# Fused image and text embedding, window attention and routed experts: two image differences of GpSimd move from slot 12 to the front of a step

## The reference, cut to what matters

```python
# x: (16, 1, 256, 256) images, x_txt: (16, 77) token ids
out = conv_general_dilated(x, KERNEL, ...)       # two 2x2 kernels: differences along the two diagonals
h = clip(sum(abs(out), axis=1), 0, 1)            # (16, 256, 256): 256 rows of a picture become 256 tokens
h = concatenate([h, take(weight, x_txt)], 1)     # 16 batches of 333 tokens, width 256
h = h + attention(layernorm(h))                  # 16 heads of 16, windows of 128 tokens, stride 64, averaged
h = h + experts(layernorm(h))                    # top 2 of 8 SwiGLU experts, 256 -> 512 -> 256
```

## Time and profile before

| what | value |
|---|---|
| median of 3 runs | 1242.64 us (1241.91 to 1243.94) |
| profiled execution, its own time | 1235.95 us |
| its span | 1233.8 us |
| mean granted clock of TensorE | 0.987 of full speed |
| busy: PE, PEld, DVE, ACT, POOL | 93%, 77%, 68%, 57%, 48% of the span |
| PE, slices of 31 us | 9 tenths or more from the third to the last but one, save 8, 7 and 8 about where the steps end |
| POOL and ACT in the last 15 slices | 2 to 3 tenths, and 1 tenth |

### The profile page before, as it was taken

The page is one execution under the profiler, slowest core; times in us unless marked ns, Lnnn a source line. Parts: engine busy times, 40 slices in busy tenths (PEclk is TensorE's granted clock), DMA queues, the critical chain, the costliest instruction groups (busy, mean ns, idle before and its releaser), DMA issues.

```text
span 1233.8 us, 34479 instructions
## 1 busy us (share of the span) xinstructions
PE 1146.1 (93%) x10510; PEld 944.6 (77%) x10511; DVE 837.9 (68%) x4279; ACT 707.0 (57%) x1979; POOL 595.6 (48%) x751
## 2 busy tenths in 40 slices
PE   2499999999999999999998798999999999999995
PEld 1366766676667667666766698999999999999995
DVE  3488899899989899989888774444444444444442
ACT  1399999999999999999999721111111111111110
POOL 7655656765676567656653362223232332323232
PEclk9799999999999999999999998999999999999998
DMA  4654446554554355434535332232333323233332
GB/s 134 180 162 122 139 136 188 142 147 131 153 144 114 96 151 147 111 99 129 148 99 173 112 101 45 47 47 47 48 47 50 47 47 47 47 47 49 49 47 30
DMA packets 98394, 123.31 MB, mean 100 GB/s; under 512 B 15544, under 2 KB 87416, under 8 KB 95192
## 3 DMA queue, kind: packets, MB, share of 16 engines
q1 hardware_dynamic: 75880, 89.96, 26.7%
q0 software_dynamic: 18576, 24.47, 12.0%
q10 hardware_dynamic: 3808, 7.34, 1.9%
HBM read 69.35 MB, written 46.07 MB: 94 GB/s over the span
## 4 chain that ended last, share of the span: by engine, by line
PE 70%; DVE 7%; ACT 7%; POOL 7%; issue 4%; SPq 2%; DMA 1%; ACTq 0%; POOLq 0%; DVEq 0%
PE t_bank L1197 13%; PE s_bank L1197 13%; PE o_bank L1212 13%; PE m_bank L1245 7%; PE t_bank L1284 6%; PE o_bank L1300 5%; ACT probs L741 4%; PE s_bank L1273 4%; DVE probs L980 3%; PE m_bank L1239 3%; PE m_bank L1397 2%; PE m_bank L1186 2%; PE o_bank L1259 1%; PE o_bank L1409 1%; ACT probsT L734 1%
## 5 line engine op out<-in xcount | busy, mean ns | idle before, releaser
L741 ACT ACTIVATE probs<-probs,neg_max 128x128 f32<-128x128 f32 x1280 | 402.4, 398 | 2.1 <-DVE neg_max L980 2.1
L980 DVE CUSTOM_DVE_ANT_0 probs<-s_bank,nbias 128x128 f32<-128x128 f32 x1280 | 293.4, 284 | 56.6 <-PE s_bank L1273 51.2
L699 ACT ACTIVATE v_all<-s_bank 128x512 f32<-128x512 f32 x91 | 54.4, 598 | 284.5 <-PE s_bank L1197 284.4
L1284 PE MATMUL t_bank<-ident,probs 128*128 128x128 f32 x1280 | 194.1, 274 | 0.2 <-ACT probs L741 0.2
L1212 PE MATMUL o_bank<-stacks,v_all 128*128 x728 | 172.7, 381 | 0.6 <-issue 0.5
L537 POOL DMA_INDIRECT out_dram<-wq_sb,nbias x46 | 75.0, 1629 | 176.5 <-DVE wq_sb L924 159.4
L734 ACT ACTIVATE probsT<-t_bank 128x512 f32<-128x512 f32 x240 | 142.0, 592 | 31.1 <-PE t_bank L1284 28.7
L537 POOL DMA_INDIRECT out_dram<-wk_sb,nbias x45 | 74.9, 1663 | 170.8 <-DVE wk_sb L924 161.9
L1212 PEld LDWEIGHTS o_bank<-stacks,v_all 128*128 128x128 f32 x728 | 131.6, 191 | 15.8 <-issue 1.7
L930 DVE TENSOR_TENSOR v_all<-v_all,t_bank 128x512 f32<-128x512 f32 x91 | 62.5, 687 | 119.0 <-PE t_bank L1197 119.0
L1300 PE MATMUL o_bank<-probsT,v_all 128*32 128x128 f32 x2560 | 136.3, 285 | 7.1 <-ACT probsT L734 4.0
(11 more groups left out here) (169 smaller groups left out, 1988.2 us busy)
## 6 DMA issues: line engine op xcount, KB each, us to landing
stacks<-qk_parts SPq DMA_DIRECT2D x192, 166.5 KB
qk_parts<-parts_flat SPq DMA_DIRECT2D x192, 83.2 KB
nbias<-expert_slots SPq DMA_DIRECT2D x91, 129.0 KB, 2.1
w_sb<-in_L_ffn_w_dram ACTq DMA_DIRECT2D x14, 512.0 KB, 3.8
v_all<-v_all SPq DMA_DIRECT2D x64, 96.0 KB
x_here<-in_x_dram SPq DMA_DIRECT2D x16, 256.0 KB
out_dram<-h_res SPq DMA_DIRECT2D x16, 256.0 KB
stacks<-in_L_ffn_w_dram SPq DMA_DIRECT2D x8, 512.0 KB, 6.0
```

The costliest lines, as they stand in the source:

```text
L741: ins = act.activation(seg, seg, ACT.Exp, bias=neg_max[:, r, i:i + 1], scale=-1.0)
L980: ins = dve.tensor_tensor_reduce(probs[:, r, i * WIN:(i + 1) * WIN], s_bank[:, k % 2, i * WIN:(i + 1) * WIN], nbias[:, h, :], 1.0, BIG, AL ...
L1284: mm = pe.transpose(t_bank[:, (k - 3) % 2, i * WIN:(i + 1) * WIN], probs[:, r, i * WIN:(i + 1) * WIN], ident[:, :])
```

## The change

In steps 0 to 12, the two subtractions of the image and their waits stand at the head of slot 0 and no longer in slot 12. In steps -3 and -1 they stay in slot 12, in step -2 in slot 17, but at the head of the slot. Steps 13 to 17 have no image, before and after.

```diff
                 for k in range(G):
+                    if pre and k == (0 if b >= 0 else 17 if b == -2 else 12):
+                        pool.wait_ge(x_in, b3 * 64 + 64)
+                        if b == -2:
+                            pool.wait_ge(xn_ready, 3)
+                        if b3 >= 1:
+                            pool.wait_ge(image_ready, b3)
+                        pool.tensor_tensor(diag[:, :, :], x_here[:, :, 0:IMG], x_below[:, :, 1:IMG + 1],
+                                           ALU.subtract).then_inc(diffs_ready, 1)
+                        pool.tensor_tensor(anti[:, :, :], x_below[:, :, 0:IMG], x_here[:, :, 1:IMG + 1],
+                                           ALU.subtract).then_inc(diffs_ready, 1)
                     v = (k - 8) // NG
...
-                    if pre and k == (17 if b == -2 else 12):
-                        pool.wait_ge(x_in, b3 * 64 + 64)
...
```

## The result

The changed kernel took 1248.6 us (median of 5 runs, 1245.87 to 1251.04), the kernel before 1242.58 us beside it (5 runs, 1241.07 to 1243.94). The ratio is 1.0050, with an interval of 1.0039 to 1.0061: 6.0 us slower. The forecast was 1240.5 us, 2.1 us faster. Of all executions in this document one, of the kernel before beside e5 to e7, took 3899.57 us and is left out of the figures as a slow run.

A forecast was written before the change was run, and what follows sets the result against it. PE stands at nine tenths; POOL's differences delay the roots, then DVE's rows and PE, with ACT late next. Gain 11 x 0.19 = 2.1 us, all else nothing: 1242.64 - 2.1 = 1240.5 us; range 1235.5 to 1244.2 us.

The forecast's parts named there:

- the roots and who holds them: Steps 2 to 12, slot 13: roots start 2.1 us sooner, DVE's 0.79 us wait goes, ACT is late next.
- The sum's only term: Steps 2 to 12: earlier roots gain 0.19 us a step, taken from imageless step 13; 11 x 0.19 = 2.1 us.
- PE's whole wait of 7.7 us: Rival: PE's whole wait for v_all in steps 2 to 12 is won, 7.7 us, giving 1234.9 us; chance 0.15.
- the gather, SP and POOL's hole: Slot 0's front: differences fit POOL's 5.05 us idle; later gather and SP's text_idx cost nothing, SP cover 1.6 us.
- the term for the picking: Front of slot 0: DVE's picking of experts beside the differences loses 0.6 us at most; put at nothing.
- last rival: Front of slot 0: differences hold DVE's picking and maxima; 1244.5 us (held for one) or 1256 us (both); chance 0.10.
- The price: DVE's picking slows at a rate of 0.6, from rows beside POOL's L581: 0.6 us at most for 1.04 us.
- The cover: Behind the picking: 0.73 us of DVE delay are covered before ACT takes DVE's maxima.
- The landing: Front of slot 0: picture lands at or before 334.5; differences at the latest from 334.5 to 336.7.
- the picking longer than 1.7 us: Sign of failure at the front of slot 0: DVE's picking of experts takes longer than 1.7 us.
- with ACT waiting behind it: Sign of failure, joined to the long picking: ACT waits behind DVE's picking.

The follow-up runs named there:

- e5: Changed kernel with the differences at the head of slot 7 in place of slot 0; 1240.40 us, ratio 0.9983 against the kernel before.
- e7: e1 plus, in steps 2 to 12, a POOL memset and a one-input scaling at the front of slot 0; 1239.61 us, ratio 0.9977.
- e6: Changed kernel, differences still ahead of the gather, but waiting for the end of DVE's picking in steps 2 and later; 1240.55 us, ratio 0.9984.
- e2: Kernel before, both subtractions kept in slot 12 and done once more at the front of slot 0 in steps 0 to 12; 1240.72 us, ratio 1.0035.
- e3: Changed kernel with the differences behind the text's gather in slot 0, without a wait for the picking; 1242.79 us, ratio 1.0059.
- e1: Changed kernel with the differences behind the gather in slot 0, in steps 2 and later also waiting for DVE's picking to end; 1233.46 us, ratio 0.9973.
- e9: The changed kernel itself run once more, against the kernel before; 1246.32 us, ratio 1.0031.
- e4: Changed kernel with only diag at the front of slot 0 and anti left in slot 12; 1234.32 us, ratio 0.9988.

## Why the prediction was wrong

**Right: the roots and who holds them.** First root 0.16 us behind the statistics (within 0.3 was asked for, and 10 of 11 steps have it); no wait of `rows` for `rstd`, none of L1390 for `v_all`; ACT's L728 as the next in line with 0.47 us; `rows` down to 1.05 us. The sum's only term, 11 x 0.19 = 2.1 us, came out as it stood: e5 and e6, which have this gain and nothing else, are 2.0 and 1.8 us faster, with periods of 40.7 to 40.8 us. Taking the gain from step 13 rather than from PE's whole wait of 7.7 us was the right choice.

**Right: the gather, SP and POOL's hole cost nothing.** e6 shows it for all of them. One duration under it was not: `text_idx` left 343.33 - 339.25 = 4.08 us behind the gather's start in step 7 of after, where the prediction carried 2.96 over, but still 3.7 us ahead of `qk_parts` (347.01).

**Wrong: the term for the picking, put at nothing.** The prediction had the place in its last rival, and let three things pass; the first is what made the sum wrong:

1. *The price.* It took a rate of 0.6 from `rows` beside L581 (0.38 us lost beside 0.64) and got "0.6 us at most" for 1.04 us of picking. But what was measured there is not a rate. A two-input operation of POOL held DVE's operations of the picking until it ended, however short they are: 0.18 us became 1.11. The delay is what is left of POOL's operation, and there are two in a row, mostly with a small DVE operation slipping in between them. The picking was late by 0.86 to 1.72 us in 10 of 11 steps, and the rival's own bound (2.17 us, held for both) was nearer than the rate. The Trainium skill says it so (SBUF — State Buffer, section "SBUF: two separate sides"): the port pair that VectorE and GpSimd share is an exclusive lock and not a split of bandwidth, the one that starts first has it for its whole instruction, and a VectorE operation with two SBUF inputs is shut out by a GpSimd operation that reads SBUF. L1022 (1.11 us), L1047 of e2 (1.02 us) and the memset of e7 (L1032 at 0.18 us) agree. L1034 of e3 (0.95 us), which reads one tensor and a column, fits only if it ran in a two-port mode, which the trace does not show. Two rows do not agree: the one-input scaling of e7 holds DVE for 0.4 of its 1.51 us, and L1037 of e3 starts 0.46 us ahead of `diag` and is held all the same.
2. *The cover.* It read 0.73 us of room before ACT's L741. The operation that was late next is PE's L1259 for `ctx_q`, with 0.65 us (0.6 in the periods). The size is nearly the same, the consumer another. The waits show it: L1259 waits for `ctx_q` behind eight pickings of after and behind none of e1, e5 and e6. Of the small delays of steps 6 and 11 (0.26 and 0.29 us lost) no wait of L1259 tells, and what passes them on was not traced.
3. *The landing.* It took the picture's landing as it was before, "at or before 334.5". This was no term of the sum, which priced a full meeting, but it decides how often they meet. SP issues that load behind the shifts of `v_all`, and the change makes just these earlier. The issue in before and then in after:

```profile
329.83 0.59 SPq L365 DMA_DIRECT2D x_here<-in_x_dram  x1
```

```profile
332.64 0.59 SPq L365 DMA_DIRECT2D x_here<-in_x_dram  x1
```

Counted from the step's L1251 it stood at 329.83 - 315.37 = 14.46 us and now stands at 332.64 - 319.53 = 13.11. The differences start 336.92 - 332.64 = 4.28 us behind the issue. With the old issue that makes 18.74 us behind L1251 (an estimate from these rows), where the picking of before is over at 18.16; with the new one 17.39, at its very start (17.41). Over steps 2 to 11 the issue stood 13.2 to 14.5 us behind L1251 in before and stands at 12.3 to 13.6 in after; in step 1, which has no wait to lose, it did not move (12.54 and 12.53). So the gain itself put most of the differences onto the picking, though not all. e2, in which the roots stay late, measures it: 4 of its 11 pickings are hit even so, against 10 of 11 in after.

**The numbers in full.** By the table, delay less 0.6 us of room, summed over the 11 steps: 8.5 us of cost. (The table's periods themselves stand 10.1 us over 11 times 40.72, the stops among them.) Less 2.1 us of gain: 6.4 us, where 6.0 were measured. The nearness is in part luck: the 0.6 was fitted to this same profile, the profile's own periods of steps 2 to 13 lost 8.0 us, and the same sum gave 5.0 for e9, where 3.1 were measured. The sum so failed in one term, 8.5 us in place of nothing. Of the forecast's signs of failure, "the picking longer than 1.7 us" came true in 10 of 11 steps, "with ACT waiting behind it" did not. The rival gave 1244.5 us (held for one) and 1256 (for both); the result lies between, outside the range, in a case that had 0.10.

## What to carry to other kernels

When work moves on GpSimd, look at what VectorE reads from SBUF at the new place, and price each meeting with a two-input GpSimd operation at the whole rest of it (here up to 1.09 us each), not at a rate; a small operation on a short path pays most. Then ask which transfers the gain itself makes earlier, since they decide whether the two meet. If they do, a wait that sets the GpSimd operation behind the short VectorE stretch costs nothing where GpSimd has a hole (e1 and e6 against e3 and after).

## What the runs showed that was not expected

- A POOL operation with two inputs (1.09 us) holds a DVE operation of 0.18 us to its end; a memset does not hold it at all; one with one input, 1.51 us long, holds it for some 0.4 us. Why the last differs is open. DVE's maxima L980, which read PSUM, keep their 0.28 us.
- In the profiles of after and of e5 to e9, but in none of before and of e1 to e4, engines stop, mostly for about 1 us, where nothing in the kernel makes them wait. In after:

```profile
DVE probsT L989 <- remote: 9.8, 10, 1.0
```

One of them in step 6, the stop of ACT behind it, and the two longest, both at once, behind the steps:

```profile
317.30 0.69 DVE L989 COPY probsT<-t_bank 128x512 f32<-128x512 f32 x1 [0.97 <-remote]
...
321.61 0.60 ACT L734 ACTIVATE probsT<-t_bank 128x512 f32<-128x512 f32 x1 [1.36 <-remote]
...
748.62 0.60 ACT L699 ACTIVATE v_all<-s_bank 128x512 f32<-128x512 f32 x1 [5.81 <-remote]
...
751.05 0.69 DVE L930 TENSOR_TENSOR v_all<-v_all,t_bank 128x512 f32<-128x512 f32 x1 [5.07 <-remote]
```

  They do not go with the change: e5 and e6 have them and are faster, e3 has none and is slower. They go with where the kernels ran: e1 to e4 ran on one chip, where the kernel before took 1236.3 us, e5 to e9 on two more, where it took 1242.4 to 1243.2 us, and beside after it took 1242.6 us. No profile of before shows the stops, so that it has them there too is read off its times alone. A stop of DVE alone costs little: e6 has periods of 40.80 to 40.83 us with one and mostly 40.71 or 40.72 without. Where ACT stops too (the periods of steps 7, 9 and 12 of after), 0.3 to 0.5 us are lost beyond the rule. So they are part of the 8.0 us by which after's periods of steps 2 to 13 exceed those of before, which is 2.0 us more than the medians differ, and probably most of the 6.7 us between before's own profile and its median; the last was not shown. What they are stays open.
